# The row maxima of a head group taken one group later on VectorE (Flamingo gated block, Trainium2)

## The reference

```python
x = x + tanh(g_xattn) * xattn(layernorm(x), ctx, ctx, W_q, W_k, W_v, W_o, query_pos, key_pos, mask)
x = x + tanh(g_ffn)   * ffn(layernorm(x), W_r, W_k, W_v, mu_r, mu_k)

# xattn, 16 heads of 32 channels, 512 queries, 120 keys
scores = Q @ K.T / sqrt(32) - slope[head] * (query_pos - key_pos);  masked places -inf
m = max(scores);  e = exp(scores - m);  attn = e / (1 + sum(e));  out = (attn @ V) @ W_o.T

# ffn: each token is mixed with the one before it
xr, xk = mu_r * x + (1 - mu_r) * x_prev, mu_k * x + (1 - mu_k) * x_prev
out = sigmoid(xr @ W_r) * (relu(xk @ W_k) ** 2 @ W_v)
```

## Time and profile before

| what | value |
|---|---|
| time, median of 3 runs | 1524.36 us (1523.87 to 1525.63) |
| span of the profiled execution | 1519.6 us |
| TensorE (PE) busy | 1442.7 us, 95% |
| VectorE (DVE) busy | 1161.5 us, 76% |
| ScalarE (ACT) busy | 889.5 us, 59% |
| GpSimd (POOL) busy | 721.3 us, 47% |
| granted TensorE clock, mean | 0.999 |

### The profile page before, as it was taken

The page is one execution under the profiler, slowest core; times in us unless marked ns, Lnnn a source line. Parts: engine busy times, 40 slices in busy tenths (PEclk is TensorE's granted clock), DMA queues, the critical chain, the costliest instruction groups (busy, mean ns, idle before and its releaser), DMA issues.

```text
span 1519.6 us, 32873 instructions
## 1 busy us (share of the span) xinstructions
PE 1442.7 (95%) x10864; PEld 1083.1 (71%) x10864; DVE 1161.5 (76%) x2889; ACT 889.5 (59%) x2928; POOL 721.3 (47%) x766
## 2 busy tenths in 40 slices
PE   7988899999999999999999999999999999999998
PEld 6876767677676767667686766767676676768667
DVE  4456868787887868798786879878687887868775
ACT  5147474665747465574747566473756657475662
POOL 0003455545455555545555464545546454555542
PEclk9999999999999999999999999999999999999999
DMA  8721001020200102020010202011020101001000
GB/s 270 215 66 49 8 29 50 0 76 0 56 20 28 49 0 76 0 56 20 28 49 14 62 0 56 20 36 41 14 62 0 56 20 53 23 27 50 1 30 28
DMA packets 53009, 65.95 MB, mean 43 GB/s; under 512 B 23024, under 2 KB 29168, under 8 KB 52976
## 3 DMA queue, kind: packets, MB, share of 16 engines
q1 hardware_dynamic: 52976, 65.52, 14.6%
HBM read 40.87 MB, written 24.64 MB: 43 GB/s over the span
## 4 chain that ended last, share of the span: by engine, by line
PE 48%; DVE 34%; issue 11%; ACT 3%; DMA 2%; DVEq 1%; SPq 0%; POOL 0%; ACTq 0%; POOLq 0%
PE rotating L401 33%; DVE probs L1038 7%; PE probs_bank L561 5%; DVE diff L1100 4%; PE score_bank L460 4%; DVE mix_k L1095 4%; PE attn_bank L575 3%; DVE relu L1100 3%; DVE square L1095 2%; PE score_bank L401 2%; ACT probs L773 2%; DVE mask_in L1137 2%; DVE stats L1008 2%; DVE norm L1017 2%; DVE xs L1064 2%
## 5 line engine op out<-in xcount | busy, mean ns | idle before, releaser
L773 ACT ACTIVATE probs<-probs,neg_max 128x120 f32<-128x120 f32 x1024 | 391.2, 385 | 29.6 <-DVE neg_max L1042 29.6
L1320 POOL TENSOR_TENSOR probs<-probs,recip 128x960 f32<-128x960 f32 x128 | 229.7, 1794 | 237.5 <-DVE recip L1053 237.5
L401 PE MATMUL rotating<-mixed_key,w_key 128*128 128x512 f32 x720 | 205.0, 413 | 24.8 <-ACT gated L825 24.8
L401 PE MATMUL rotating<-w_proj,attn_t 128*128 128x512 f32 x768 | 220.9, 417 | 2.9 <-DVE xnt_or_act L1023 2.0
L781 ACT COPY probs_t<-probs_bank 120x512 f32<-120x512 f32 x256 | 149.8, 585 | 121.3 <-PE probs_bank L561 121.1
L1038 DVE SCALAR_TENSOR_TENSOR probs<-mask_in,score_bank 128x120 f32<-128x120 f32 x1024 | 213.0, 269 | 9.5 <-PE score_bank L460 9.5
L401 PE MATMUL rotating<-w_value,xnt_or_act 128*128 128x512 f32 x720 | 202.3, 409 | 10.2 <-DVE xs L1064 10.2
L401 PE MATMUL rotating<-w_gate,mixed_gate 128*128 128x512 f32 x768 | 209.7, 409 | 0.0
L401 PE MATMUL rotating<-xnt_or_act,w_query 128*128 128x256 f32 x1536 | 198.7, 286 | 0.5 <-DVE xnt_or_act L1023 0.5
L773 ACT ACTIVATION_READ_ACCUMULATOR probs<-probs,neg_max 128x1 f32 x1024 | 194.0, 189 | 0.0
L401 PEld LDWEIGHTS rotating<-xnt_or_act,w_query 128*128 128x128 f32 x1536 | 187.7, 191 | 1.9 <-DVE xnt_or_act L1023 0.8
(11 more groups left out here) (126 smaller groups left out, 2167.7 us busy)
## 6 DMA issues: line engine op xcount, KB each, us to landing
xs<-in_x_dram SPq DMA_DIRECT2D x64, 256.0 KB, 2.9
out_dram<-gated SPq DMA_DIRECT2D x64, 256.0 KB, 3.0
value_scratch<-gated SPq DMA_DIRECT2D x16, 240.0 KB, 2.6
mask_in<-in_mask_dram SPq DMA_DIRECT2D x16, 240.0 KB, 2.6
keys_t<-key_scratch SPq DMA_DIRECT2D x16, 240.0 KB, 3.6
values<-value_scratch SPq DMA_DIRECT2D x16, 240.0 KB, 3.8
probs<-in_ctx_t_dram SPq DMA_DIRECT2D x6, 480.0 KB, 7.0
key_scratch<-query_t SPq DMA_DIRECT2D x12, 240.0 KB, 5.1
```

The lines of the kernel that those rows point to most:

```text
L401: mm = pe.matmul(bank, stationary(a, c), moving(b, c), start=(i == 0), stop=(i == MATMULS - 1))
L773: e = act.activation(probs[:, t % 2, head, :], probs[:, t % 2, head, :], ACT.Exp, bias=neg_max[:, t % 2, head:head + 1], accum_out=sums[:, ...
L1320: pool.tensor_tensor(part, part, recip[:, t % 2, heads].unsqueeze(2).to_broadcast((P, H // 2, NK)), ALU.mult)\
```

## The change

The maximum leaves `bias` and becomes a function of its own, `maximum`, with the same wait and the same instruction. In VectorE's order the maximum of a group is put behind the biases of the next group (in tile 3, the one of group 1 goes behind `normalise1` and the one of group 3 behind the statistics and the reciprocals), and some biases go ahead of a residual. ScalarE's, GpSimd's, TensorE's and SyncE's orders stay as they are.

```diff
                 z.then_inc(scores_biased, 1)
+
+            def maximum(b, t, g):
                 dve.wait_ge(scores_biased, (b * QT + t) * G + g + 1)
                 dve.tensor_reduce(neg_max[:, t % 2, g * J:(g + 1) * J], probs[:, t % 2, g * J:(g + 1) * J, :],
                                   AX.X, ALU.max, negate=True).then_inc(max_ready, 1)
...
-                for g in range(G):
+                bias(b, 0, 0)
+                for g in range(1, G):
                     bias(b, 0, g)
+                    maximum(b, 0, g - 1)
+                maximum(b, 0, 3)
                 reciprocals(b, 0, 0)
                 reciprocals(b, 0, 1)
-                for g in range(G):
+                bias(b, 1, 0)
+                for g in range(1, G):
                     bias(b, 1, g)
+                    maximum(b, 1, g - 1)
+                maximum(b, 1, 3)
                 attn_low(b, 0)
                 reciprocals(b, 1, 0)
                 bias(b, 2, 0)
+                bias(b, 2, 1)
+                maximum(b, 2, 0)
                 residual(b, 0)
                 reciprocals(b, 1, 1)
-                bias(b, 2, 1)
                 bias(b, 2, 2)
+                maximum(b, 2, 1)
                 bias(b, 2, 3)
+                maximum(b, 2, 2)
+                maximum(b, 2, 3)
                 statistics2(b, 0)
...
                 reciprocals(b, 2, 1)
                 bias(b, 3, 0)
                 bias(b, 3, 1)
+                maximum(b, 3, 0)
                 after((normalise1, 0))
+                maximum(b, 3, 1)
                 bias(b, 3, 2)
+                bias(b, 3, 3)
+                maximum(b, 3, 2)
                 residual(b, 1)
                 statistics2(b, 1)
                 reciprocals(b, 3, 0)
-                bias(b, 3, 3)
+                maximum(b, 3, 3)
                 feed_forward((finish, 2))
```

## The result

| | before | after |
|---|---|---|
| time, median of 20 runs | 1524.34 us (1520.84 to 1526.17) | 1526.22 us (1523.53 to 1529.65) |
| ratio, 95% interval | | 1.0016 [1.0009, 1.0023] |
| span of the profiled execution | 1519.6 us | 1524.9 us |
| loop, 14 batches in the trace | 1229.8 us | 1232.3 us |

The ratio is + 2.4 us (+ 1.4 to + 3.5); the forecast of + 1.4 us lies at the lower end of that. The change is a small loss, just inside the 0.2% that was called no change. Wherever an execution has both its time and its span on record, the time is 1.8 us above the span. So 3.0 of the 4.8 us between before's median and its profiled span mean that this execution was a quicker one than the median.

The account below looks back on a forecast made before the run. TensorE bounds the kernel, with at most 24 us of its waits to regain; 14 x 0.12 = + 1.7 us, first batch - 0.4, last + 0.1, together + 1.4, gave 1525.8 us, own range 1523.5 to 1528.5 (chance 0.70).

Parts of the forecast that it names:

- The price of a wait on the operation just before: VectorE, each maximum behind its own biases: the wait costs 0.12 us, 1.9 us a batch, 31 us in all.
- Rival (a): VectorE: the 0.12 us gap stays ahead of every maximum, nothing saved; + 6 us, 1530.4 us, chance 0.12.
- Tile 0: PE's 0.91 us wait at tile 1's scores goes, but later exponentials make the fourth turn of probabilities 0.16 us late.
- rival (c): Splits' chain in tile 0 has more play, so PE keeps the whole first wait; - 12 us, 1512.5 us, chance 0.08.
- Tile 3: First maximum behind a second bias group delays ScalarE by 0.63 us; PE loses 0.60 at tile 2's second turn.
- rival (b): Tile 3's normalisation waits for GpSimd's difference, 1.9 us instead of 0.65; + 19 us, 1543.6 us, chance 0.05.
- Value 3: Starts at the later of PE's side, + 0.06 us, and VectorE's residual 2, + 0.13; taken as + 0.12 a batch.
- The sum: Whole kernel: 14 loop batches + 1.7 us, first batch - 0.4, last + 0.1; together + 1.4, giving 1525.8 us.
- First batch: Batch ahead of the loop: the wait ahead of tile 1's scores is kept as a gain, - 0.4 us.
- The last batch: Batch behind the loop: + 0.1 us.

Follow-up runs that it names:

- t0_only: New order of maxima in tile 0 alone, tiles 1 to 3 as in the original kernel; ratio to the original 1.0015.
- tile0_later: Changed kernel with tile 0's first maximum one more bias group late, behind the biases of group 2; ratio to the original 1.0074.
- tile0_first: Changed kernel with tile 0's first maximum put back directly behind its own biases, tile 3 as changed; ratio to the original 0.9966.
- finish_early: Changed kernel with finish 3 moved ahead of the statistics 2 on VectorE; ratio to the original 0.9990.
- before_again: The original kernel, unaltered, run and profiled a second time; ratio to its first run 1.0002.
- first_now: Changed kernel with the first maxima of tiles 0 and 3 directly behind their own biases again, one tile 2 maximum moved too; 1506.98 us, ratio to the original 0.9885.
- again: The changed kernel, unaltered, run and profiled a second time; ratio to the original 1.0016.
- tile3_first: Changed kernel with tile 3's first maximum put back directly behind its own biases, tile 0 as changed; ratio to the original 0.9951.

## Why the prediction was right, and where its sum was not

**The price of a wait on the operation just before: right.** 0.12 us a group was predicted and measured (1.44 to 1.32). The forecast took it from an overlap of 0.08 us seen wherever nothing waited. Over the kernel VectorE has 21.9 us less busy time, and the 8.8 us that it idled ahead of maxima before are gone: 30.7 us, where 31 were forecast (the busy time also holds a few operations that changed for another reason, below). Rival (a), by which nothing is saved, falls. (Its price of 0.42 us a batch was not the later of its own two terms, 0.33 and 0.49; by 0.49 it would have been 1531.2 us.)

The Trainium skill's rule that was weighed there (VectorE: DVE Perf Modes, "The DRAIN you can't avoid") says that the semaphore costs nothing extra. That is not so here: where the operation in front is the one that is waited for, the next starts 0.12 us later than where it is not. But the prediction took the section for stricter than it is. The sentence rests there on eight copies in a row, and the same section says that a next operation that is not held back starts earlier, with which the 1.32 us agree.

**Tile 0: right.** PE's 0.91 us wait went and did not pay: + 0.16 was predicted at the fourth turn, + 0.15 measured as a median and + 0.19 in the batch shown. t0_only carries it through to the period, tile0_later shows that no play is left. The new PE wait, put at about 0.7 us at the fourth turn, came in two: 0.51 at the third for GpSimd and 0.36 at the fourth. So rival (c) falls too. For another order it would have been half right: in tile0_first the fourth turn comes 0.40 us earlier than before.

**Tile 3: right.** + 0.76 was predicted at tile 2's second turn, + 0.71 measured (+ 0.74 in the batch shown), with ScalarE's wait at 2.03 us (about 2.0 predicted) and a new PE wait of 0.41 (0.6 predicted). The normalisation slipped into the gap ahead of GpSimd's difference (0.67 us, predicted 0.65), so rival (b) falls.

**Value 3: both terms mis-sized.** The sum took the later of PE's side (+ 0.06) and VectorE's (+ 0.13) and came to + 0.12; measured is - 0.24. Both sides were better than told. First three rows of before: PE's transpose ahead of value 3; VectorE's second half of a mix (line 1100); the GpSimd operation beside it.

```profile
769.55 0.66 PE L484 MATMUL rotating<-ident,norm 128*128 128x128 f32 x4
```

```profile
766.26 1.94 DVE L1100 SCALAR_TENSOR_TENSOR diff<-diff,mu,xn2t 128x128 f32<-128x128 f32 x4
```

```profile
766.75 1.04 POOL L1341 TENSOR_TENSOR relu<-xn2t 128x512 f32<-128x512 f32 x1
```

The same mix after the change:

```profile
770.18 1.14 DVE L1102 SCALAR_TENSOR_TENSOR diff<-diff,mu,xn2t 128x128 f32<-128x128 f32 x4
```

On PE the sum set 0.76 us lost against the 0.70 us of wait at 770.90, and the wait was worth more. In before the transpose starts at 769.55 and value 3 at 770.90, 1.35 us apart; in after the two stand 774.47 - 774.06 = 0.41 apart. So 0.94 us could be had, not 0.70: the 0.70 is counted from the modelled end of those matmuls, the spacing of starts is what PE needs. That gives PE 0.76 - 0.94 = - 0.18.

That alone would not have moved the forecast, as VectorE's + 0.13 was the later one. VectorE was as late as forecast up to the end of finish 2 (49.64 us after key 0 as a median, 49.52 before: + 0.12). Then the prediction had it that nothing waits up to residual 2. But in before the mix at 766.26 lies on GpSimd's operation of 766.75 and takes 1.94 us; in after that operation starts at 771.45, when the mix of 770.18 is over, and the mix takes 1.14 (the same in all 14 batches of either kernel to 0.02 us). The normalisation behind it takes 0.94 instead of 0.53. So residual 2 starts 57.93 us after key 0, 58.19 before: - 0.26, where + 0.13 was forecast. That the GpSimd operation is what stretches the mix was read from the rows, not tried.

**A step that was missing: the gain given back.** The prediction stopped at value 3. Behind it after loses 0.42 us of period (value 3 to the next key 0: 28.84 in before, 29.26 in after). In the batch shown VectorE's normalisation at 776.02 takes 1.47 us, 0.77 in before, and lies on this GpSimd operation:

```profile
775.92 1.29 POOL L1366 TENSOR_TENSOR mixed_gate<-diff,mixed_gate 128x512 fp32r<-128x512 f32 x1
```

The normalisation starts 0.10 us behind it and ends 0.28 behind its end, at 777.49. Over the 14 batches this normalisation takes 0.75 to 0.77 us in before and t0_only, and 1.28 to 1.50 in every kernel with a new order in tile 3. Behind it stands `finish` (62.69 us after key 0, 62.14 before), behind that the load of x (issued at 780.18), the statistics at 783.13 that wait 1.09 us for it, and the transpose for which PE waits in ten batches. finish_early cuts this chain at one place and the 0.37 us come back. That the GpSimd operation stretches the normalisation was read from the rows, not tried. The Trainium skill (SBUF — State Buffer, "Who interferes with whom") names the port that the two engines share, with the one that issues first blocking the other; the rows agree.

**First batch: tile 3's loss was left out.** The sum had - 0.4 there, for the scores of tile 1. PE's transposes of line 491 and tile 2's second turn, in before_again and then in after, two executions whose granted clock is the same in each of nine stretches from 90 to 186 us:

```profile
138.35 1.11 PE L491 MATMUL rotating<-ident,norm 128*128 128x128 f32 x4 [2.17 <-DVE gated L1129]
...
144.45 0.62 PE L561 MATMUL probs_bank<-ident,probs 128*120 128x128 f32 x4
```

```profile
136.96 1.11 PE L491 MATMUL rotating<-ident,norm 128*128 128x128 f32 x4 [2.17 <-DVE gated L1131]
...
143.68 0.62 PE L561 MATMUL probs_bank<-ident,probs 128*120 128x128 f32 x4 [0.40 <-ACT probs_t L781]
```

The turn comes 6.10 us behind the transposes in before_again and 6.72 in after. All six executions with before's place for tile 3's first maximum have 6.08 to 6.13, all six with the new one 6.72 or 6.73. This is the 0.60 that the prediction worked out for the loop; it had even named this wait in the first batch (141.32), and did not enter it. The gain of 0.4 depends on the clock. Line 491's transposes come 40.95 us behind the first scores in before, and 40.41 to 40.43 in the five other executions that were granted 1.00 over 97 to 106 us (all with the new order in tile 0, or with first_now's), a gain of 0.5 against before's single one; in the six that were granted 0.81 there, before_again among them, they come after 42.04 to 42.08, and nothing is gained. From the first scores to the loop's first key 0, after takes 92.80 us and before_again 91.80: + 1.0, not - 0.4.

**The sum.** Per batch + 0.18 us measured (88.02 - 87.84), + 0.12 predicted. That the size is right is luck: two errors nearly cancel, 0.36 too late at value 3 and 0.42 not seen behind it. Over the loop + 2.5 us (predicted + 1.7). The first batch has + 1.0 (predicted - 0.4) where it was granted 0.81 over 97 to 106 us. The last batch, from its key 0 to the start of PE's last group of products, took 89.75 us (89.71 before; + 0.1 was predicted). Together + 3.5 us, at the upper end of what the runs allow (+ 1.4 to + 3.5); an execution with the clock at 1.00 in the first batch gains half a microsecond of that back.

**Better than both: first_now.** 1506.98 us, 1.15% under before. It keeps the order of the change for most of the later groups, where the maximum has time, and puts the first maximum of tiles 0 and 3, for which ScalarE idles, directly behind its biases.

## What to carry to other kernels

To take an operation away from behind the one that it depends on saves its own wait (0.12 us here), and costs its consumer the whole time of what is put between (0.75 us, less the 0.12). So it pays only for results that nobody waits for yet: move the later ones of a group, leave the first. A wait in the list of an engine's waits is worth the spacing of its instructions' starts. At tile 1's scores the two agree (0.91 us printed, 3.93 - 3.01 = 0.92 by starts), at value 3, behind short transposes, they don't (0.70 and 0.94). And a sum that ends where the last wait goes is not finished: follow what the other engines do until the next period starts, which of their operations now lie on each other, and the buffers and loads too. What was worked out for the loop holds for the batch written out ahead of it as well.

## What the runs showed of the hardware

The granted clock in the first batch differs between executions of one and the same kernel. PE in two stretches (window, us, busy us and number of matmuls, granted clock, DMA share, GB/s), first before, then before_again, then after:

```profile
97.00:106.00 9.00, 8.36 (x74) 1.00 0.40 118
136.00:144.00 8.00, 6.73 (x42) 1.00 0.12 31
```

```profile
97.00:106.00 9.00, 7.25 (x66) 0.81 0.37 118
136.00:144.00 8.00, 5.83 (x31) 0.79 0.27 74
```

```profile
97.00:106.00 9.00, 8.16 (x59) 0.81 0.36 118
136.00:144.00 8.00, 6.64 (x27) 0.79 0.15 40
```

At 1.00 the clock is at its higher level, 2.4 GHz; 0.81 and 0.79 are stretches that hold some time at the lower one, 1.2 GHz. again shows 0.81 and 1.00, tile3_first 1.00 and 0.82. So each of these two stretches can fall in one execution and hold in another of the same kernel; the kernel does not decide it. Ahead of the first stretch PE idles 1.75 or 1.76 us in all three executions, and what falls in it are 48 matmuls. They start at 97.21 us in before and take 5.62 us; in before_again and in after they start at 99.23 and 97.84 and take 7.23.

From the first scores to the first key 0 of the loop before took 90.67 us in one execution and 91.80 in the other, after 92.80 and 92.67. So 1.1 of the 2.1 us between the two profiles of the first table are the clock (40.95 and 42.04 us up to line 491's transposes), and 1.0 is the change, as told above. The rest of the 5.3 us between the two profiled spans: 0.6 ahead of the first scores, where ScalarE waits longer for a load (14.97 us, 14.01 before), 2.5 in the loop, and 0.04 at the end.
